# Routing tokens group by group and sending their rows to per-expert regions with indirect DMA, in place of a routing stage with selection matmuls

## The chip, the cores and the metric

The kernel runs on one core of one Trainium2 chip. The metric is the device time of one execution in microseconds (us). The engines named below are PE (TensorE, matmuls and transposes), PEld (its weight loads), DVE (VectorE), ACT (ScalarE), POOL (GpSimd, which also issues the indirect DMAs) and SP (SyncE, which issues all other DMAs). Each engine works through its own list of instructions in order and waits on semaphores. TensorE's clock has two levels, 1.2 and 2.4 GHz; the profile gives the granted clock as a share of the full one.

## What is computed

An attention block is followed by a mixture-of-experts block, on 4 batches of 2048 tokens with 256 features (8192 tokens). Cut to what matters:

```python
x = x + layernorm(attn(layernorm(x)))     # 16 heads; the 16x16 attention is over feature channels
u = layernorm(x); h = layernorm(u) * ln_g + ln_b           # 8192 tokens
logits = h @ Wr                                             # 7 routed experts
top_vals, top_idx = top_k(logits, 2); gates = softmax(top_vals)
idx = top_idx.T.reshape(-1)               # all first choices, then all second choices
pos = running count of earlier entries with the same expert; keep = pos < 732
xe[e, pos] = h[token]                     # 7 experts x 732 slots, the rest is dropped
ye = (silu(xe @ W1) * (xe @ W3)) @ W2     # 256 -> 1024 -> 256 per expert
routed[token] += ye[e, pos] * gate
shared = (silu(h @ W1s) * (h @ W3s)) @ W2s                  # all tokens
x = x + layernorm(routed + shared)
```

The order of the queue matters: an expert's 732 slots are filled by first choices over all 8192 tokens, and then by second choices.

## The kernel before

**Tiles and stages.** Tokens go in 16 groups of 512 (4 tiles of 128 rows; `GT` = 4), 4 groups per batch (`GB`). Every FFN matmul is done as three (high times low parts; `three`, lines 975 to 977). The stages, in order of time:

1. Attention of batch 0 alone (the opening).
2. A loop of three rounds, `Fori(1, B)`: in round b the shared FFN of the four groups of batch b-1 (four *chunks*, each with 8 steps m = 0..7) runs beside the attention of batch b.
3. Two more shared chunks (12 and 13), with the last steps of the attention of batch 3 and then the routing of all tokens.
4. 14 expert chunks (7 experts, two parts of 3 tiles each), whose rows are fetched by `gather` and whose results are added into `y_scratch` by `scatter`.
5. The two held shared chunks (14 and 15), beside the last layernorm, which goes on to the end.

**What sets the order.** A timetable written by hand. A round has 64 *places*: each of the 32 steps m has an even place (after `up(m)` on PE, after the product `act` on DVE) and an odd one (after `down(m-2)` on PE, after `low(m-1)` on DVE). `timetable` says at which place each step of the attention stands, `attend` issues it on each engine that has a part in it, and `LEAD` = 8 moves it: place p of a batch's timetable is place p + 8 of the round, and places 56 to 63 stand at the start of the next round. Per group q the timetable has x_stats, x_norm, x_turn0, x_low0, x_turn1, x_gram at 4q+1 to 4q+7; then the channel attention (m_gram at 20 to m_low at 37, with m_turn at 22, m_sym at 23, m_times_wqk at 24); then o_mix, o_stats, o_norm, o_add, u_stats, u_norm, u_turn0, u_turn1, u_route at 38+4q plus 0, 1, 3, 4, 6, 9, 10, 11, 12.

**Names that the change and the steps below touch.** The step keys "m_turn" and "m_sym" are on DVE `m_sum` (line 1248) and `m_sym` (line 1253): they sum the Gram matrix into `gf`, the first half of buffer `u`. PE's `m_times_wqk` (line 1015) reads that. `x_rstd` (line 655) and `x_part` (line 660) are POOL's parts of x_stats and x_low0, `x_norm` (line 1226) needs the former. `u_norm` (line 1325) writes the normed rows to `u`; SP stores them to `u_scratch` (`store_u`, line 499). `u_route` makes the logits on PE (line 1077) and copies them on DVE to `lg` (line 1332). The product `act` is line 1358, `act_lo` line 1351, the low part of a chunk's input line 1345.

**Routing before.** After all logits are there, the places after the attention in chunks 12 and 13 hold it (`route`): DVE takes the best two experts, counts, scans and positions over 448 columns (lines 1399 to 1463); PE's `count` adds up; then 32 blocks follow, each with two comparisons on DVE (`select`, lines 1475 and 1477), two products on POOL (lines 696, 697) and four fp32 matmuls on PE (line 1179), which together build a table of token number and gate per slot. `indices` (lines 1483 to 1489) reads it out, and only then `gather` (line 713) can fetch the first expert's rows. `scatter` is line 737. POOL also makes the six low parts of the first expert's weights (`low_piece`, line 651).

## Time and profile before

| what | value |
|---|---|
| median of 3 runs | 1268.76 us (1264.95 to 1269.63) |
| the profiled execution | 1270.08 us, its span 1268.3 us |
| PE busy | 1128.9 us, 89% |
| DVE busy | 724.9 us, 57% |
| ACT busy | 519.3 us, 41% |
| POOL busy | 391.4 us, 31% |
| mean granted clock | 0.941 |
| shares of the chain that ended last | PE 72%, DVE 9%, issue 8%, POOL 6%, ACT 3%, DMA 2% |

Busy PE is not PE at its peak: matmuls are pipelined and overlap in the records, so a matmul's own duration is longer than the distance to the next. In the timelines and in the chain times are us from the start of the span; ns stand where "min/median/max" is written. A bracket at the end of a timeline row says how long the engine was idle before it and what released it. Waits that are named are inferred from semaphores.

### The profile page before, as it was taken

To read this page: it belongs to the slowest core of one execution; us is meant where nothing else is said; L and a number is where in the kernel's file an instruction comes from. 1 tells how busy PE (TensorE), PEld (TensorE's weight loads), DVE (VectorE), ACT (ScalarE), POOL (GpSimd) and SP (SyncE) were. 2 spreads that over 40 slices of the span, in tenths; PEclk is the share of its full clock that TensorE was granted. 3 is DMA by queue.
4 is the path that set the end of the run, shared out by engine and by line. 5 is a ranking of instruction groups with operands and counts; after the bars stand their busy time and mean duration, and the time that the engine had idled before them with its cause. 6 is when DMAs were issued, how large, how long until landed. Compare 5 with 4: busy or idle time off the path is not lost.

```text
span 1268.3 us, 20395 instructions
## 1 busy us (share of the span) xinstructions
PE 1128.9 (89%) x6932; PEld 1033.2 (81%) x6932; DVE 724.9 (57%) x1541; ACT 519.3 (41%) x916; POOL 391.4 (31%) x321
## 2 busy tenths in 40 slices
PE   3557999999999999999998698999999999999760
PEld 2456888988888888888887597999999999998650
DVE  4445684464764564845667994445354454454885
ACT  2313343434434344343444212545455455453543
POOL 4523120131210230300312485144343434213554
PEclk9566999999999999999998898999999999999985
DMA  4206212044110044110353103244253242255773
GB/s 141 83 17 226 74 51 67 13 145 177 52 52 30 34 151 151 67 51 17 103 180 100 34 1 111 81 119 113 47 129 91 73 124 54 42 163 163 237 260 130
DMA packets 84004, 125.38 MB, mean 99 GB/s; under 512 B 8645, under 2 KB 68553, under 8 KB 83921
## 3 DMA queue, kind: packets, MB, share of 16 engines
q1 hardware_dynamic: 73728, 113.80, 27.0%
q0 software_dynamic: 10192, 10.52, 4.9%
q8 instruction: 47, 0.77, 0.3%
q14 instruction: 37, 0.30, 0.1%
HBM read 76.30 MB, written 47.98 MB: 98 GB/s over the span
## 4 chain that ended last, share of the span: by engine, by line
PE 72%; DVE 9%; issue 8%; POOL 6%; ACT 3%; DMA 2%; SPq 1%; POOLq 0%; ACTq 0%; DVEq 0%
PE bank L975 21%; PE bank L976 21%; PE bank L977 21%; PE bank L997 2%; PE bank L1077 2%; POOL sb_t_scale L772 2%; DVE sb_st L1206 1%; PE bank L1179 1%; PE bank L1069 1%; DVE sb_x L1477 1%; POOL sb_x L436 1%; ACT sb_ln_o L817 1%; PE bank L987 1%; DVE sb_act L1358 1%; PE bank L1015 1%
## 5 line engine op out<-in xcount | busy, mean ns | idle before, releaser
L1358 DVE TENSOR_TENSOR sb_act<-bank,sb_act 128x512 f32<-128x512 f32 (+2 forms) x240 | 148.7, 620 | 406.5 <-PE bank L977 365.8
L975 PE MATMUL bank<-sb_h_hi,sb_wup_lo 128*128 128x512 f32 (+2 forms) x960 | 354.8, 370 | 18.1 <-DVE sb_h_lo L1345 9.1
L976 PE MATMUL bank<-sb_h_lo,sb_wup_hi 128*128 128x512 f32 (+2 forms) x960 | 351.0, 366 | 0.0
L977 PE MATMUL bank<-sb_h_hi,sb_wup_hi 128*128 128x512 f32 (+2 forms) x960 | 349.6, 364 | 0.0
L899 ACT ACTIVATE sb_act<-bank 128x512 f32<-128x512 f32 (+2 forms) x240 | 130.1, 542 | 477.0 <-PE bank L977 434.2
L975 PE MATMUL bank<-sb_wdn_hi,sb_act_lo 128*128 128x256 f32 (+1 forms) x848 | 252.6, 298 | 24.4 <-DVE sb_act_lo L1351 22.4
L977 PE MATMUL bank<-sb_wdn_hi,sb_act_hi 128*128 128x256 f32 (+1 forms) x848 | 241.2, 284 | 0.0
L976 PE MATMUL bank<-sb_wdn_lo,sb_act_hi 128*128 128x256 f32 (+1 forms) x848 | 241.0, 284 | 0.0
L975 PEld LDWEIGHTS bank<-sb_h_hi,sb_wup_lo 128*128 128x128 f32 x960 | 183.9, 192 | 36.6 <-issue 11.9
L977 PEld LDWEIGHTS bank<-sb_h_hi,sb_wup_hi 128*128 128x128 f32 x960 | 182.9, 191 | 22.0
L976 PEld LDWEIGHTS bank<-sb_h_lo,sb_wup_hi 128*128 128x128 f32 x960 | 183.9, 192 | 16.3
L1351 DVE TENSOR_TENSOR sb_act_lo<-sb_act,sb_act_hi 128x512 fp32r<-128x512 f32 (+2 forms) x240 | 181.6, 757 | 13.2 <-ACT sb_act_hi L871 12.5
L975 PEld LDWEIGHTS bank<-sb_wdn_hi,sb_act_lo 128*128 128x128 f32 (+1 forms) x848 | 161.1, 190 | 32.7 <-DVE sb_act_lo L1351 31.1
L976 PEld LDWEIGHTS bank<-sb_wdn_lo,sb_act_hi 128*128 128x128 f32 (+1 forms) x848 | 161.8, 191 | 1.5
L977 PEld LDWEIGHTS bank<-sb_wdn_hi,sb_act_hi 128*128 128x128 f32 (+1 forms) x848 | 161.4, 190 | 0.0
L871 ACT ACTIVATE sb_act_hi<-sb_act 128x512 fp32r<-128x512 f32 (+2 forms) x240 | 136.4, 569 | 1.8 <-DVE sb_act L1358 1.8
L737 POOL DMA_INDIRECT y_scratch<-sb_ysb,sb_scur x42 | 76.7, 1827 | 161.2 <-ACT sb_ysb L888 126.7
L665 POOL TENSOR_TENSOR sb_rstdB<-sb_veB,sb_mhalf 128x4 f32<-128x4 f32 x16 | 16.2, 1015 | 231.9 <-DVE sb_veB L1305 231.9
L713 POOL DMA_INDIRECT sb_rows<-u_scratch,sb_gcur x42 | 46.7, 1112 | 57.2 <-PE bank L1093 38.9
L660 POOL TENSOR_TENSOR sb_wdn_hi<-sb_xn,sb_wdn_hi 128x1024 fp32r<-128x1024 f32 x16 | 38.2, 2389 | 57.4 <-ACT sb_wdn_hi L785 57.4
L655 POOL TENSOR_TENSOR sb_rstd<-sb_veA,sb_mhalf 128x4 f32<-128x4 f32 x16 | 16.1, 1008 | 103.0 <-DVE sb_veA L1217 103.0
L670 POOL TENSOR_TENSOR sb_x<-sb_ln_o,sb_x 128x1024 f32<-128x1024 f32 x16 | 38.1, 2381 | 30.4 <-ACT sb_ln_o L817 30.4
(195 smaller groups left out, 1452.5 us busy)
## 6 DMA issues: line engine op xcount, KB each, us to landing
sb_xin<-in_L_ffn_W_dram SPq DMA_DIRECT2D x28, 512.0 KB
sb_xin<-in_L_attn_x_dram SPq DMA_DIRECT2D x16, 512.0 KB, 3.6
sb_x<-in_L_attn_x_dram SPq DMA_DIRECT2D x16, 512.0 KB, 5.1
x_scratch<-sb_x SPq DMA_DIRECT2D x16, 512.0 KB, 5.7
u_scratch<-sb_u SPq DMA_DIRECT2D x16, 512.0 KB, 3.2
hT_scratch<-sb_hr SPq DMA_DIRECT2D x16, 512.0 KB, 2.8
sb_hfull<-hT_scratch SPq DMA_DIRECT2D x16, 512.0 KB, 3.9
y_scratch<-sb_ysb SPq DMA_DIRECT2D x14, 512.0 KB, 2.8
```

The costliest lines, as they stand in the source:

```text
L660: v.tensor_tensor(xx[:, :, 1, :], xn[:, :, :], xx[:, :, 0, :].bitcast(F32), ALU.subtract).then_inc(xlo_ok, 1)
L670: v.tensor_tensor(x2[:, q % 2, :, :], ln_o[:, :, :], x2[:, q % 2, :, :], ALU.add).then_inc(x2_ok, 1)
L713: pool.indirect_dma_start(rows[0:w, part, t, :], None, u_d, bass.IndirectOffsetOnAxis(ap=gcur[0:w, part, t:t + 1], axis=0)).then_inc(gathe ...
L737: pool.indirect_dma_start(y_d, bass.IndirectOffsetOnAxis(ap=scur[0:w, part, t:t + 1], axis=0), ysb[0:w, part, t, :], None, compute_op=ALU. ...
L772: v.tensor_tensor(t_scale[g % 2], veA[:, :], mhalf[:, :], ALU.pow).then_inc(t_rstd, 1)
L871: s.activation(act_hi[:, m % 4, 0:c.w], act[:, m % 2, 0:c.w], ACT.Copy).then_inc(ahi_ok, 1)
L899: s.activation(act[:, m % 2, 0:c.w], a[:, 0:c.w], ACT.Silu).then_inc(silu_ok, 1)
L975: t_.matmul(o, a_lo, b_hi, start=start, stop=False, skip_group_check=True)
L976: t_.matmul(o, a_hi, b_lo, start=False, stop=False, skip_group_check=True)
L977: return t_.matmul(o, a_hi, b_hi, start=False, stop=stop, skip_group_check=True)
L1351: v.tensor_tensor(act_lo[:, m % 4, 0:c.w], act[:, m % 2, 0:c.w], act_hi[:, m % 4, 0:c.w].bitcast(F32), ALU.subtract).then_inc(alo_ok, 1)
L1358: v.tensor_tensor(act[:, m % 2, 0:c.w], bank[(4 if c.wide and m % 2 else 0) + 1][:, 0:c.w], act[:, m % 2, 0:c.w], ALU.mult).then_inc(act_o ...
```

## The change

Routing is done per group of 512 tokens, beside the attention. Three steps are new in the timetable. DVE's `u_route` picks both choices of its 4 tiles right after the logits and writes the difference of the two values into column `GAP` of the group's rows; `u_norm` writes the token number into column `TOK` (rows are now 258 wide). PE's `u_count` (place 52 + 4q) counts with 11 small bf16 matmuls, and DVE's `u_slot` (same place) turns the counts, with a running `carry`, into a row number in `sent_scratch`, which has a region of 768 rows per expert and choice. POOL's `u_send0` to `u_send3` then send each tile's 128 rows twice, with one indirect DMA per tile and choice: 8 per group. These stand at places 57, 61, 84 and 88 (plus the tile's number) for the groups 0 to 3 of a batch. The timetable now reaches place 119, so that the last two groups' sends of a batch stand at places 28 to 35 of the next round.

The selection stage, its tables and the store of `u` go. `indices` shrinks to four small operations; an expert's slots read first the region of first choices, and from its end on that of second choices. The gate is computed per expert part from `GAP` (`exps` on POOL, `gates` on DVE), the scatter's targets from `TOK`. `sent_scratch` is first filled with rows that carry a spare token number: 15 DMAs on SP's queue in the opening. Group q's normed rows stand in four buffers (`early`, the two halves of `rows`, `u`) instead of one. x_turn0, x_turn1, u_turn0 and u_turn1 now share one PSUM bank in the rounds. The low parts of the first expert's weights move from POOL to DVE.

```diff
@@ timetable
-                             ("u_norm", 9), ("u_turn0", 10), ("u_turn1", 11), ("u_route", 12)):
+                             ("u_norm", 9), ("u_turn0", 10), ("u_turn1", 11), ("u_route", 12), ("u_count", 14),
+                             ("u_slot", 14)):
                 timetable[38 + 4 * q + at].append((name, q))
+        for q, at in enumerate((57, 61, 84, 88)):
+            for t in range(GT):
+                timetable[at + t].append((f"u_send{t}", q))
@@ SP, the opening
+                if place == CLEAR_AT[0]:
+                    sp.dma_start(sent_d[2 * E * ROOM:, :].rearrange("(n p) w -> p n w", p=P),
...
+                if place in CLEAR_AT:
+                    sp.dma_start(sent_t[CLEAR_AT.index(place)], zrow[:, :].rearrange("p (a w) -> p a w", a=1
+                                 ).broadcast_to([P, ST, UW])).then_inc(none_in, 16)
@@ POOL
+            def u_send(t):
+                def step(b, q):
+                    if t == 0:
+                        pool.wait_ge(r_slot, OPEN + b * GB + (q + 1))
+                        if isinstance(b, int) and b == 0 and q == 0:
+                            pool.wait_ge(none_in, (2 * E + 1) * 16)
+                        elif q > 0:
+                            pool.wait_ge(sent[q - 1], b * SENT + SENT)
+                        else:
+                            pool.wait_ge(sent[GB - 1], b * SENT)
+                        pool.sem_inc(pool_go, 1)
+                    for c in range(2):
+                        pool.indirect_dma_start(sent_d, bass.IndirectOffsetOnAxis(ap=sendto[:, q, t, c:c + 1], axis=0),
+                                                u[q][:, t, :], None).then_inc(sent[q], 16)
+                return step
...
-            for j in range(PIECES):
-                low_piece(1, j, 1, stage_later)
-
-            pool.wait_ge(r_slots, 1)
-            for n in range(NBLK):
...
-                v.tensor_tensor(selB[:, r, :, 0, :], selE[:, r, :, :], along(tokid[:, cut], NC), ALU.mult)
-                v.tensor_tensor(selB[:, r, :, 1, :], selE[:, r, :, :], along(gates[:, c, cut], NC),
-                                ALU.mult).then_inc(r_sel, 1)
@@ PE
+            def u_count(b, q):
+                pe.wait_ge(r_oh, b * GB + (q + 1))
+                t_.matmul(counts, earlier[:, :], oh[:, :, :, :].rearrange("p t c e -> p (t c e)"),
+                          start=True, stop=False, skip_group_check=True)
...
+                for t in range(1, GT):
+                    for s in range(t):
+                        t_.matmul(counts[:, t * 2 * E:(t + 1) * 2 * E], onesb[:, :], of[s],
+                                  start=False, stop=False, skip_group_check=True)
+                for t in range(GT):
+                    ins = t_.matmul(totals, onesb[:, :], of[t], start=False, stop=(t == GT - 1),
+                                    skip_group_check=True)
...
-                    for t in range(RB):
-                        ins = t_.matmul(bank[6][:, 0:2 * NC], selA[:, n % SR, t, :],
-                                        selB[:, n % SR, t, :, :].rearrange("p a c -> p (a c)"),
...
@@ DVE, m_sum
                 dve.wait_ge(m_act, OPEN + b * MA + 1)
-                dve.wait_ge(u_out, OPEN + b * (16 * GB))
+                if not (isinstance(b, int) and b == 0):
+                    dve.wait_ge(sent[GB - 1], b * SENT)
@@ DVE, u_route (new part) and u_slot
+                for c in range(2):
+                    ch.link(v.tensor_reduce(best[:, c, :], lg[:, :, :], AX.X, ALU.max))
+                    ch.link(v.tensor_tensor(same[:, :, :], lg[:, :, :], over_e(best[:, c, :]), ALU.is_equal))
+                    ch.link(v.tensor_tensor(same[:, :, :], same[:, :, :], of_e, ALU.mult))
+                    ch.link(v.tensor_reduce(first[:, :], same[:, :, :], AX.X, ALU.max))
+                    ins = v.tensor_tensor(oh[:, :, c, :], same[:, :, :], over_e(first[:, :]), ALU.is_equal)
...
+            def u_slot(b, q):
...
+                dve.wait_ge(r_cnt, g + 1)
+                ch.link(v.tensor_tensor(place_of[:, :, :, :], counts.rearrange("p (t c e) -> p t c e", c=2, e=E), over_t,
+                                        ALU.add))
...
+                ch.link(v.tensor_reduce(pos[:, :, :], place_of[:, :, :, :], AX.X, ALU.add))
+                ch.step(v.tensor_copy(sendto[:, q, :, :], pos[:, :, :]))
+                ch.settle()
+                dve.sem_inc(r_slot, 1)
@@ DVE, per expert part
+            def gates(c):
...
+                ch.link(v.tensor_scalar(gsum[:, :], ex, 1.0, None, ALU.add))
+                ch.link(v.reciprocal(grec[:, :], gsum[:, :]))
...
@@ DVE, chunks 12 and 13
-            def select(n):
...
-                v.tensor_tensor(selE[:, r, :, :], across(colid[:, :], NC), along(slotcol[:, c, cut], NC),
-                                ALU.is_equal).then_inc(r_selE, 1)
-                v.tensor_tensor(selA[:, r, :, :], across(slot1[:, :], P), along(slotm[:, c, cut], P),
-                                ALU.is_equal).then_inc(r_selA, 1)
```

Where the sends stand is told by the order of the instructions. POOL, in a round, from the end of x_low0 of the batch's last group to the first step after it. Before:

```order
L655 TENSOR_TENSOR sb_rstd<-sb_veA,sb_mhalf 128x4 [waits a_var]
L659 REGISTER_ALU
L660 TENSOR_TENSOR sb_wdn_hi<-sb_xn,sb_wdn_hi 128x4x256 [waits xhi_ok]
L665 TENSOR_TENSOR sb_rstdB<-sb_veB,sb_mhalf 128x4 [waits b_var]
L669 ISA [waits lno_ok]
```

and with the change:

```order
L683 TENSOR_TENSOR sb_rstd<-sb_veA,sb_mhalf 128x4 [waits a_var]
L687 REGISTER_ALU
L688 TENSOR_TENSOR sb_wdn_hi<-sb_xn,sb_wdn_hi 128x4x256 [waits xhi_ok]
L707 REGISTER_ALU
L716 DMA sent_scratch<-sb_rows,sb_sendto 11776x258 [waits r_slot,sent1]
L716 DMA sent_scratch<-sb_rows,sb_sendto 11776x258 x7
L707 REGISTER_ALU
L716 DMA sent_scratch<-sb_u,sb_sendto 11776x258 [waits r_slot,sent2]
L716 DMA sent_scratch<-sb_u,sb_sendto 11776x258 x7
L693 TENSOR_TENSOR sb_rstdB<-sb_veB,sb_mhalf 128x4 [waits b_var]
```

Sixteen indirect DMAs, for groups 2 and 3 of the batch before, now stand between x_low0 and the next step, and group 3's wait until group 2's have landed (`sent2`).

DVE, in a round, around the sum of the Gram matrix into `u`. Before:

```order
L1358 TENSOR_TENSOR sb_act<-bank,sb_act 128x512 [waits b_ps,silu_ok]
L1244 ISA
L1245 ISA [waits m_act]
L1248 TENSOR_TENSOR sb_u<-sb_ln_o 128x512 [waits ut_ps,u_out]
L1351 TENSOR_TENSOR sb_act_lo<-sb_act,sb_act_hi 128x512 [waits dn_done,ahi_ok]
L1253 TENSOR_TENSOR sb_u<-sb_u,bank 128x512 [waits m_pe]
```

and with the change:

```order
L1478 TENSOR_TENSOR sb_act<-bank,sb_act 128x512 [waits b_ps,silu_ok]
L1286 ISA
L1288 REGISTER_ALU [waits m_act]
L1291 TENSOR_TENSOR sb_u<-sb_ln_o 128x512 [waits ut_ps,sent3]
L1454 TENSOR_TENSOR sb_act_lo<-sb_act,sb_act_hi 128x512 [waits dn_done,ahi_ok]
L1294 ISA
L1295 REGISTER_ALU [waits m_chain]
L1296 TENSOR_TENSOR sb_u<-sb_u,bank 128x512 [waits m_pe]
```

The operations are the same; the first now waits for `sent3`, the landing of group 3's sends of the batch before, where it waited for the store of `u`.

## Rows read from the trace of the kernel before

**Rows 1.** Windows: from:to, length, busy time of each engine, clock, DMA share, GB/s.

```profile
295.20:473.80 178.60, 174.42 (x1063) 154.92 (x1061) 102.96 (x243) 72.60 (x122) 32.62 (x20) 1.00 0.25 84
446.90:459.90 13.00, 13.00 (x93) 12.09 (x93) 8.94 (x28) 5.18 (x10) 4.86 (x3) 1.00 0.62 203
652.40:786.10 133.70, 112.87 (x699) 100.68 (x697) 102.93 (x159) 35.89 (x55) 68.36 (x80) 0.92 0.20 67
```

**Rows 2.** Timeline of DVE, chunks 12 and 13: start, length, line, operation.

```profile
655.29 0.69 DVE L1358 TENSOR_TENSOR sb_act<-bank,sb_act 128x512 f32<-128x512 f32 x1 [3.47 <-PE bank L977]
775.89 0.69 DVE L1358 TENSOR_TENSOR sb_act<-bank,sb_act 128x512 f32<-128x512 f32 x1 [3.04 <-PE bank L977]
```

**Rows 3.** The chain that ended last, two stretches: start, length, what.

```profile
377.48 0.12 PE bank L975
...
381.66 1.73 PE bank L1015 x8
...
779.86 2.67 DMA sb_rows<-u_scratch,sb_gcur
782.58 0.56 PE bank L1093 x3
...
787.06 0.69 PE bank L975
```

**Rows 4.** Forms of one line's instructions: ns min/median/max, first and last start.

```profile
L1077 PE MATMUL bank<-sb_wr,sb_hr x256: 169/255/378, 97.4 to 669.9; 128*128 128x7 f32 x128
L1160 PEld LDWEIGHTS bank<-sb_oh,sb_onesb x2: 96/96/96, 679.7 to 694.5; 128*128 128x128 bf16 x2
```

**Rows 5.** The page's groups of indirect DMAs on POOL: busy, mean ns, idle before.

```profile
L737 POOL DMA_INDIRECT y_scratch<-sb_ysb,sb_scur x42 | 76.7, 1827 | 161.2 <-ACT sb_ysb L888 126.7
L713 POOL DMA_INDIRECT sb_rows<-u_scratch,sb_gcur x42 | 46.7, 1112 | 57.2 <-PE bank L1093 38.9
```

**Rows 6.** Timeline of POOL in a round, at chunk 12 and in the experts.

```profile
304.48 1.02 POOL L674 TENSOR_TENSOR sb_rstd<-sb_ve,sb_mhalf 128x4 f32<-128x4 f32 x1 [12.93 <-DVE sb_ve L1317]
323.85 1.01 POOL L655 TENSOR_TENSOR sb_rstd<-sb_veA,sb_mhalf 128x4 f32<-128x4 f32 x1 [18.35 <-DVE sb_veA L1217]
362.12 2.40 POOL L660 TENSOR_TENSOR sb_wdn_hi<-sb_xn,sb_wdn_hi 128x1024 fp32r<-128x1024 f32 x1 [4.36 <-ACT sb_wdn_hi L785]
658.10 1.02 POOL L674 TENSOR_TENSOR sb_rstd<-sb_ve,sb_mhalf 128x4 f32<-128x4 f32 x1 [9.87 <-DVE sb_ve L1317]
783.08 0.95 POOL L713 DMA_INDIRECT sb_rows<-u_scratch,sb_gcur  x1 [0.30 <-issue]
832.19 0.58 POOL L705 COPY sb_gcur<-sb_gidx 128x3 uint32<-128x3 uint32 x1 [4.30 <-DMA y_scratch<-sb_ysb,sb_scur]
```

**Rows 7.** Timeline of DVE in a round, and small chained operations in `indices`.

```profile
325.82 1.38 DVE L1226 TENSOR_SCALAR sb_xn<-sb_xin,sb_mv,sb_rstd 128x256 f32<-128x256 f32 x4
377.76 0.68 DVE L1248 TENSOR_TENSOR sb_u<-sb_ln_o 128x512 f32<-128x512 f32 x1
378.96 0.68 DVE L1253 TENSOR_TENSOR sb_u<-sb_u,bank 128x512 f32<-128x512 f32 x1
772.19 0.20 DVE L1486 TENSOR_TENSOR sb_tabe<-sb_tabe,sb_spare 128x42 f32<-128x42 f32 x1
772.43 0.20 DVE L1488 TENSOR_TENSOR sb_tabe<-sb_tabe,sb_table 128x42 f32<-128x42 f32 x1
```

**Rows 8.** Timeline of PE: the first x_turn0 of a round.

```profile
328.53 0.60 PE L987 MATMUL bank<-sb_ident,sb_xn 128*128 128x128 f32 x4
```

**Rows 9.** Windows after PE's wait for the first expert's rows; columns as in rows 1.

```profile
790.00:792.00 2.00, 2.00 (x7) 2.00 (x7) 0.56 (x1) 0.00 (x0) 0.57 (x2) 0.50 1.01 302
792.00:794.00 2.00, 2.00 (x12) 2.00 (x12) 0.04 (x1) 0.91 (x2) 0.00 (x0) 0.94 0.99 313
```

**Rows 10.** Timeline of the opening: SP issues the residual loads, POOL first uses one.

```profile
48.94 0.93 SPq L485 DMA_DIRECT2D sb_x<-in_L_attn_x_dram  x2
85.37 2.36 POOL L670 TENSOR_TENSOR sb_x<-sb_ln_o,sb_x 128x1024 f32<-128x1024 f32 x1 [2.24 <-ACT sb_ln_o L817]
```

**Rows 11.** Window with SP's queue full; columns as in rows 1.

```profile
298.00:302.00 4.00, 4.00 (x21) 3.39 (x22) 0.34 (x1) 2.24 (x3) 0.00 (x0) 1.00 0.99 299
```

More of the change, by code:

```diff
@@ L246, in sandwich_kernel @@
         u_ok = sem("u_ok")
-        u_out = sem("u_out")
+        sent = [sem(f"sent{i}") for i in range(GB)]
         ut_ps = sem("ut_ps")
@@ L350, in held_chunks, with stored @@
         def held_chunks(body, between=lambda place: None):
[L352 to L353 removed]
+            seq = [expert_chunk(E - 1, 1, 1)] + [held_chunk(h) for h in range(HELD)] + [None]
+            for h in range(HELD):
+                body(seq[h], seq[h + 1], seq[h + 2], lambda place: between(2 * FM * h + place))
+        def stored(s):
+            return sum((n + HELD) % 2 == s for n in range(FIRST))
         NCH = NG + 2 * E
@@ L559, in _ @@
             b = B - 1
-            load_h(b, 1)
-            for place in range(PLACES - LEAD, PLACES):
-                attend(steps, place, b)
             for k in range(4):
@@ L565, in _ @@
                 sp.sem_inc(sp_go, 1)
-            for j in range(PIECES):
+            for j in range(3):
+                load_piece(1, j, [W1[0], W3[0]], W2[0], stage_later)
+            if HELD < GB - 1:
+                load_h(b, 1)
+            for place in range(PLACES - LEAD, TIMES):
+                attend(steps, place, b)
+            for j in range(3, PIECES):
                 load_piece(1, j, [W1[0], W3[0]], W2[0], stage_later)
@@ L597, in _ @@
                 sp.dma_start(last_y[k], last_view(y_d[0:T, :], k)).then_inc(t_y[k], 16)
+            for h in range(2, HELD):
+                load_held(h)
             for g in range(NG):
@@ L743, in _ @@
             gather(0, 1)
+            exps(0, 0, 0)
+            exps(0, 1, 0)
             release(0, 0)
@@ L1491, in route @@
-            def route(place):
-                for step, c in routing.get(place, ()):
-                    step(c)
-                for n in blocks_at(place):
-                    select(n)
-                if place == R_IDX:
-                    indices()
-            cs = last_chunks()
-            body(None, cs[0], cs[1], lambda place: beside_last(steps, route, place))
-            body(cs[0], cs[1], None, lambda place: beside_last(steps, route, 2 * FM + place))
-            low(cs[1], FM - 1)
@@ new lines, in route @@
+            def route(place):
+                if place % 2 and 5 <= place < 5 + 2 * PIECES:
+                    j = (place - 5) // 2
+                    if j == 4:
+                        dve.wait_ge(sent[0], B * SENT)
+                    low_piece(1, j, 1, stage_later)
+                if place == INDEX_AT:
+                    indices()
+            cs = [None] + last_chunks() + [None]
+            for j in range(1, len(cs) - 1):
+                body(cs[j - 1], cs[j], cs[j + 1], lambda place: beside_last(steps, route, 2 * FM * (j - 1) + place))
```

516 lines of the change are left out of this document (250 added, 266 removed).

## The prediction, made before the changed kernel ran

> **What bounds the kernel now.** I read the busy times first: PE is busy for 89% of the span, no other engine for more than 57%. Then the windows: inside a round PE is busy in 174.4 of 178.6 us at full clock while DVE has 103 us of work, but in the stretch from the end of the rounds to the first expert chunk (133.7 us) PE has 112.9 us, DVE 102.9 us, and the granted clock falls to 0.92 [rows 1]. So the kernel is bound by PE nearly everywhere, and in the routing stretch by DVE, POOL and PE in turn. The chain of waits says how that stretch ends: the gather of the first rows lands, PE turns them, and the first expert matmul starts at 787.06 [rows 3]. The question is what that stretch becomes without its selection, and what its work costs where PE was full.
>
> **Term 1, the routing stretch: -52.5 us.** One step m of a shared chunk costs PE 4.18 us (381.66 less 377.48: one `down` and one `up` with nothing between) [rows 3]. The first product of chunk 12 is at 655.29, the last of chunk 13 at 775.89 [rows 2]. Between them lie 15 steps, 62.7 us. The tail of the attention adds two sets of logits (16 records each, about 1.7 us for a set: 0.105 us apart, with a median of 255 ns for one because they overlap [rows 4]), eight transposes (0.7 us) and three new counts (0.8 us each, below), together 6.5 us; for DVE running late I add 2 us. So the last product comes at 726.5. From there to the first expert matmul it was 11.2 us, of which about 3 us was PE waiting for the gather (rows landed at 782.5); the rest stays: 734.6. Gain 787.06 less 734.6, 52.5 us. What hides the sends here: POOL is free from 659.1 [rows 6], four groups at 13.3 us each (term 2) end at 712, and gather takes 6 us more, so the rows are there at 718, before PE asks at about 729. DVE has the six low parts of the weights as new work (about 1.2 us each, one per step), in steps where it has over 2 us free.
>
> **Term 2, the sends: +48 us.** The trace has no plain indirect write. Nearest are the gather, 0.95 us where nothing disturbs it [rows 6] and 1.112 us in the mean of 42, and the accumulating scatter, 1.827 us [rows 5]; 0.30 us lies between two [rows 6]. I take the gather's mean, since both move a row without arithmetic, and the accumulation is what the scatter has more: 1.41 us per send, 11.3 us per group. A group must land before the next starts: 1.7 us after the gather's issue (landing 2.67 us after its start) [rows 3], 4.3 us after the scatter's [rows 6]; I take 2.0. A group is then 13.3 us (bounds 11.7 and 21.3).
>
> The Trainium skill, page "SBUF — State Buffer", section "SBUF: two separate sides", says that a DVE operation in a two-port mode keeps GpSimd from writing descriptors until it ends. The spread between 0.95 us and the mean of 1.112 us is the only thing here that fits it; by the undisturbed price this term would be about 7 us smaller. No run here separates the two.
>
> First place, the start of a round: POOL is free at 305.5, sends groups 0 and 1 until 305.5 + 13.3 + 11.3 = 330.1, and only then does x_rstd, which stood at 323.85 [rows 6]. x_norm waits for that, 1.4 us long [rows 7], and x_turn0 on PE stood at 328.53 [rows 8]. It would start at 332.5; new work ahead moves everything here by some 2 us, so 2 us are lost, 6 us in three rounds.
>
> Second place, which decides: POOL ends the last x_part at 364.5 [rows 6], sends groups 2 and 3 (row order above) and they have landed at 364.5 + 26.6 = 391.1. `m_sum` on DVE stood at 377.76 and now waits for that. Queued behind it on DVE are act_lo and m_sym, and `m_times_wqk` on PE, at 381.66 [rows 3], needs m_sym. The three take 1.9 us (0.6 us from start to start) [rows 7], so PE goes on at 393.0 and has stood for 11.3 us. After an idle PE the clock is at its lower level: PE's dense work at 787.06 ran at 0.50, the level of 1.2 GHz, until about 792 [rows 9], 5 us of work at half speed, 2.6 us lost. Together 13.9 us, in three rounds 41.7 us.
>
> **Term 3, routing beside the FFN: +21.5 us.** A count is 11 bf16 matmuls with 11 weight loads. Bounds from two rows: 0.105 us apart like the logits' fp32 records [rows 4], 1.16 us; half that, as the bf16 weight load takes 96 ns where the fp32 one takes 190, 0.58 us. I take 0.8 us. On DVE a group gets 10 new operations in u_route and 8 in u_slot at 0.24 us from start to start (0.2 us each, chained) [rows 7], and two small copies: 4.6 us. DVE has 8.94 us of work in 13.0 us in the fullest window [rows 1], so the sum is 13.5 us where PE's becomes 13.8: both full, and DVE in order. Where logits stand ahead of act_lo and u_norm, I find u_norm about 0.7 us after the point where PE wants to transpose. I take 1.0 us per group. 1.8 us times 12 groups in the rounds is 21.6 us (bounds 0.6 and 3.5 per group: 7 and 42).
>
> **Term 4, the opening: +5.5 us.** There the path runs through DVE, so the two u_route chains (2.4 us each) and part of a u_slot count: 5 us. SP fills `sent_scratch` ahead of the residual loads: 13 of the 15 DMAs, 10240 rows of 1032 bytes, 10.6 MB. At the 299 GB/s of a full queue [rows 11] that is 35 us; they start when the residual loads did, 48.9, and these then land at about 86 to 88, where 85.4 was wanted [rows 10]. 0.5 us, bounds 0 and 15 (a rate a third lower).
>
> **Nothing: the experts.** Per part POOL gets one `pow` (1 us) and DVE one copy and four small operations, 1.2 us of 25 us. PE has two PSUM banks per product there and is busy without a break; the cover is DVE's half-idle time. Bounds -2 and +6. The rest of the tail is untouched.
>
> **Sum.** 1268.3 - 52.5 + 48 + 21.5 + 5.5 = 1290.8 us of span; the execution was 1.8 us longer than its span, so 1292.6, and 1.3 us less against the median of the runs: 1292.
>
> **Rivals.**
> (a) The stretch gained outweighs the rest (faster). Mechanism: the wait of m_sum. Its loss per round is 364.5 + two groups + 1.9 - 381.7. With the lowest price (1.25 us per send, 1.7 us to land) that is 8.1 us without a fall of the clock; with counts and chains at 0.6 us per group and 2 us in the opening the sum is -55 + 24 + 7 + 2 = -22, 1247. The point from which it decides: with my other terms the whole breaks even at a loss of 6 us per round, a send of 1.08 us with its gap. For it: 0.95 us stands in the trace. Against: even that with its gap is 1.25.
> (b) A plain indirect write costs what the accumulating one does (1.83 + 0.3 us, 4.3 to land, 21.3 per group). Then m_sum loses 27.3 + 2.6 us per round, x_norm about 18, and the sends of chunks 12 and 13 end at 744, so that the first rows come 20 us after PE could take them: 52.5 becomes 32. Sum -32 + 90 + 54 + 21.5 + 5.5: about 1407. For it: same direction, SBUF to memory. Against: packets and bytes are the same, only the addition differs.
> (c) The middle is worse than taken: DVE is the bound in all 16 groups (3.5 us each) or the filling holds up the residual loads. +20 or +15: about 1310.
>
> **How the numbers follow.** Forecast (1275 to 1305) 0.47; (a), 1245 to 1275, 0.25; (b) 0.10; (c), with sends half-way between the two prices, 0.18. The range 1252 to 1340 leaves out (b) and the low end of (a). About 0.5%, 6 us, is what a measurement can tell from no change. Faster by more than that (below 1262) is most of (a), 0.20; same (to 1275) the rest of it and the forecast's lower edge, 0.12; slower 0.68.
>
> **What would show it.** Right: in each round DVE's sum into `sb_u` idle for 9 to 14 us behind an indirect DMA, PE idle as long ahead of its line, and the clock low after it; sends of 1.0 to 1.2 us, 128 of them; a round of 193 to 203 us in place of 178.6; 80 us from chunk 12 to the first expert. Wrong: a send near 1.8 us, an experts' stretch that grows, or PE full through the middle of a round.

## The result, and the profile after

The changed kernel took 1326.17 us (median of 4, 1324.05 to 1328.51), the kernel before 1267.53 us (its three earlier runs and one more): a ratio of 1.046, 95% interval 1.044 to 1.049, slower by 58.6 us. The forecast was 1292 us. The direction held and the time lies in the range, but the loss is more than twice the 24 us forecast. The experiments below split it in two: run on two other chips, the same program takes 1299.5 and 1301.9 us, so 24 to 27 us of the 58.6 are not in the program alone. Two single executions, one of the kernel before and one of `e4_again`, took over 1860 us at a granted clock of 0.56 and are left out of all times. I therefore show two traces of it, *after* (the first measurement, span 1324.4 us) and *c0* (the same program on another chip, span 1300.7 us).

To see where time goes I compare the starts of the same `up` product on PE in two traces. In the kernel before, the first products of the three rounds start at 117.1, 298.0 and 476.6, that of chunk 12 at 652.3, the first expert product at 787.06 [rows 3], one late in the experts at 1089.2. A *mark* below is the first `up` product of any step m; it shifts by what it falls further behind the kernel before, counted from the mark ahead of it. Differences of the stretches to before, in us:

| kernel | opening | three rounds | of it at m_sum | chunk 12 to experts | experts | tail | span |
|---|---|---|---|---|---|---|---|
| forecast | +5.5 | +69.2 | +41.7 | -52.5 | 0 | 0 | +22.5 |
| after | +9.9 | +89.7 | +35.5 | -45.9 | +2.1 | +0.1 | +56.0 |
| c0 | +10.5 | +71.5 | +35.4 | -52.5 | +1.8 | +1.1 | +32.4 |

The tail is what is left to the span's end. Windows of after (round 2 and the last stretch), then of c0; the columns are those of rows 1:

```profile
336.20:544.70 208.50, 183.85 (x1102) 160.03 (x1102) 117.06 (x327) 73.00 (x123) 64.25 (x52) 0.95 0.24 82
751.90:840.80 88.90, 77.51 (x473) 66.55 (x471) 42.82 (x109) 32.97 (x52) 45.59 (x46) 0.98 0.42 138
```

```profile
331.90:533.60 201.70, 180.99 (x1102) 158.30 (x1102) 117.35 (x327) 73.18 (x124) 64.61 (x52) 0.97 0.25 84
734.30:816.60 82.30, 75.71 (x474) 65.54 (x472) 42.69 (x109) 33.08 (x52) 45.17 (x46) 0.99 0.47 149
```

A round was 178.6 us with PE busy for 174.4 [rows 1]. In c0 it is 201.7 us, and PE stands for 20.7 of them. DVE has 14 us more work in 84 more instructions, POOL 32 us more, the sends. The last stretch was 133.7 us and is 82.3: the gain that was forecast is there.

**The wait that decided.** c0, round 2: the timelines of POOL, DVE and PE (start, length, what; in brackets the idle time before it and what ended it):

```profile
402.94 2.39 POOL L688 TENSOR_TENSOR sb_wdn_hi<-sb_xn,sb_wdn_hi 128x1024 fp32r<-128x1024 f32 x1 [4.47 <-ACT sb_wdn_hi L836]
418.81 0.96 POOL L716 DMA_INDIRECT sent_scratch<-sb_u,sb_sendto  x1 [2.70 <-issue]
427.66 0.96 POOL L716 DMA_INDIRECT sent_scratch<-sb_u,sb_sendto  x1 [0.30 <-issue]
430.11 0.69 DVE L1291 TENSOR_TENSOR sb_u<-sb_ln_o 128x512 f32<-128x512 f32 x1 [11.25 <-DMA sent_scratch<-sb_u,sb_sendto]
432.05 3.78 PE L1067 MATMUL bank<-sb_wqk,sb_u 128*128 128x256 f32 x8 [9.35 <-DVE sb_u L1296]
```

The last x_part ends at 405.33. Groups 2 and 3 go out and have landed at 430.1, 24.8 us later, and only then may DVE sum the Gram matrix into `u`. PE stands for 9.35 us, and behind it the eight matmuls of L1067 take 3.78 us, where rows 3 have 1.73: the clock is at its lower level (0.54 in the window from 432 to 437, 1.00 in the next five). Together the same product comes 11.9 us later.

**The price of a send.** The row of c0's trace for half of the sends, those out of buffer `rows` (ns min/median/max, first and last start), and three rows of its timelines:

```profile
L716 POOL DMA_INDIRECT sent_scratch<-sb_rows,sb_sendto x64: 956/961/1741, 153.2 to 784.3; - x64
```

```profile
414.59 0.69 DVE L1454 TENSOR_TENSOR sb_act_lo<-sb_act,sb_act_hi 128x512 fp32r<-128x512 f32 x1
414.92 1.19 POOL L716 DMA_INDIRECT sent_scratch<-sb_rows,sb_sendto  x1 [0.30 <-issue]
415.20 1.22 DVE L1448 TENSOR_TENSOR sb_h_lo<-sb_hfull,sb_h_hi 128x1024 fp32r<-128x1024 f32 x1
```

105 of the 128 sends take 0.96 to 0.99 us, the mean is 1.01. Of the 23 longer ones 19 begin while DVE subtracts one SBUF tile from another (act_lo, the low part of a weight): here act_lo ends at 415.28 and the send at 416.11, 0.83 us later, and that distance is the same in 16 of them (0.91 in three). The next subtraction, which starts 0.28 us into the send, does not hold it. Of the other sends under such a subtraction three begin in its last 0.14 us, and three begin 0.02 us behind its start and are not held. The eleven sends that begin under DVE's product out of PSUM (L1478) all take 0.96 us. The Trainium skill, page "SBUF — State Buffer", section "SBUF: two separate sides", has this as a lock on a port pair, held by whichever starts first, and names DVE operations with two SBUF inputs among those that take it, against a GpSimd operation that reads SBUF. The 19 held sends and the eleven agree with that, the three at the start of a subtraction do not. The 19 cost 6.3 us of POOL's time in all.

**The opening.** SP's and POOL's timelines, c0:

```profile
49.52 29.23 SPq L555 DMA_DIRECT2D sent_scratch<-sb_zrow  x12
79.36 3.47 SPq L497 DMA_DIRECT2D sb_x<-in_L_attn_x_dram  x2
90.46 2.34 POOL L698 TENSOR_TENSOR sb_x<-sb_ln_o,sb_x 128x1024 f32<-128x1024 f32 x1 [7.51 <-DMA sb_x<-in_L_attn_x_dram]
```

The residual loads went out at 48.94 before and POOL used one at 85.37 [rows 10]. Now twelve clearing DMAs hold SP for 29 us, and POOL waits 7.5 us for the load.

**The turn of a round.** c0, from round 1 to round 2, ACT, DVE and PE:

```profile
318.91 1.93 ACT L869 ACTIVATE sb_ln_o<-bank,sb_nbiasB,sb_rstdB 128x256 f32<-128x256 f32 x4 [2.28 <-DVE sb_nbiasB L1352]
321.36 0.69 DVE L1478 TENSOR_TENSOR sb_act<-bank,sb_act 128x512 f32<-128x512 f32 x1 [2.48 <-ACT sb_act L954]
321.97 0.18 DVE L1385 COPY sb_lg<-bank 128x28 f32<-128x28 f32 x1
325.24 0.16 DVE L1399 TENSOR_TENSOR sb_rows<-sb_best 128x4 f32<-128x4 f32 x1
325.31 0.68 DVE L1454 TENSOR_TENSOR sb_act_lo<-sb_act,sb_act_hi 128x512 fp32r<-128x512 f32 x1
326.05 0.58 PE L1026 MATMUL bank<-sb_wdn_hi,sb_act_lo 128*128 128x256 f32 x1 [4.24 <-DVE sb_act_lo L1454]
336.75 0.66 PE L1122 MATMUL bank<-sb_ident,sb_rows 128*128 128x128 f32 x4 [1.03 <-ACT sb_hr L878]
346.63 0.66 PE L1122 MATMUL bank<-sb_ident,sb_u 128*128 128x128 f32 x4 [1.57 <-DVE sb_u L1375]
```

DVE's slot chain ahead (314.16 to 315.90) makes the norm's bias late (ACT waits 2.28 us for it), ACT's silu comes behind that, DVE's product behind the silu, and then DVE works through the choice of experts, from 321.97 to 325.40, before act_lo. PE waits 4.24 us for it, and its granted clock is 0.50 from 326.0 to 330.5, where it was 1.00 at this place before. Before, the same two waits were 0.45 and 0.27 us.

In c0 the marks shift by 4.0, 3.4 and 5.1 us at the three turns. At the next mark they shift by 1.2 to 1.6 us: the second transposes of a group wait 1.03 us for the bank that they share with the first. Two marks further the shift is 2.1 us in each round: at 346.63 PE waits for u_norm, which stands on DVE behind the next choice of experts. A count adds 0.4 us. At the start of the attention two transposes share a bank again, and the shift is 1.2 to 1.3 us.

### The profile page after: what moved, and what is told of

Its sections match the earlier page's. It is cut to its first block, busy times and chain, and to the rows that moved or that the text cites. A ratio compares the mean times of both kernels' runs of the same rounds, so it can differ in the third digit from the quotient of the medians.

```text
span 1324.4 us, 20814 instructions
## 1 busy us (share of the span) xinstructions
PE 1121.6 (85%) x6848; PEld 1013.3 (77%) x6848; DVE 718.9 (54%) x1847; ACT 517.0 (39%) x913; POOL 471.3 (36%) x380
## 4 chain that ended last, share of the span: by engine, by line
PE 36%; issue 6%; POOL 5%; DVE 2%; DMA 1%; ACT 1%; another core or an unknown queue 0%; POOLq 0%; ACTq 0%; DVEq 0%; SPq 0%
PE bank L1026 12%; PE bank L1028 11%; PE bank L1027 11%; POOL sb_t_scale L823 2%; POOL sent_scratch L716 1%; POOL sb_x L448 1%; PE bank L1161 1%; POOL y_scratch L782 0%; DMA sb_xin<-in_L_ffn_W1s_dram 0%; DMA y_scratch<-sb_ysb,sb_scur 0%; DVE sb_act_lo L1454 0%; DVE sb_st L1248 0%; DMA sb_xin<-y_scratch 0%; POOL sb_rows L448 0%
## 5 line engine op out<-in xcount | busy, mean ns | idle before, releaser
L1478 DVE TENSOR_TENSOR sb_act<-bank,sb_act 128x512 f32<-128x512 f32 (+2 forms) x240 | 148.8, 620 | 406.2 <-PE bank L1028 308.5
L1028 PE MATMUL bank<-sb_h_hi,sb_wup_hi 128*128 128x512 f32 (+2 forms) x960 | 353.3, 368 | 0.0
L1028 PE MATMUL bank<-sb_wdn_hi,sb_act_hi 128*128 128x256 f32 (+1 forms) x848 | 244.0, 288 | 0.0
L1454 DVE TENSOR_TENSOR sb_act_lo<-sb_act,sb_act_hi 128x512 fp32r<-128x512 f32 (+2 forms) x240 | 175.1, 729 | 17.8 <-ACT sb_act_hi L923 13.0
L751 POOL DMA_INDIRECT sb_rows<-sent_scratch,sb_gcur x42 | 48.6, 1157 | 104.3 <-DVE sb_scur L1444 47.2
L716 POOL DMA_INDIRECT sent_scratch<-sb_rows,sb_sendto x64 | 67.4, 1054 | 34.1 <-issue 24.3
L702 POOL TENSOR_TENSOR sb_rstd<-sb_ve,sb_mhalf 128x4 f32<-128x4 f32 x16 | 19.9, 1245 | 97.9 <-DVE sb_ve L1360 97.9
```

The lines of the kernel that those rows point to most:

```text
L716: pool.indirect_dma_start(sent_d, bass.IndirectOffsetOnAxis(ap=sendto[:, q, t, c:c + 1], axis=0), u[q][:, t, :], None).then_inc(sent[q], 16)
L751: pool.indirect_dma_start(rows[0:w, part, t, :], None, sent_d, bass.IndirectOffsetOnAxis(ap=gcur[0:w, part, t:t + 1], axis=0)).then_inc(ga ...
L1028: return t_.matmul(o, a_hi, b_hi, start=False, stop=stop, skip_group_check=True)
L1454: v.tensor_tensor(act_lo[:, m % 4, 0:c.w], act[:, m % 2, 0:c.w], act_hi[:, m % 4, 0:c.w].bitcast(F32), ALU.subtract).then_inc(alo_ok, 1)
L1478: v.tensor_tensor(act[:, m % 2, 0:c.w], bank[(4 if c.wide and m % 2 else 0) + 1][:, 0:c.w], act[:, m % 2, 0:c.w], ALU.mult).then_inc(act_o ...
```

## The experiments

Edits are to the changed kernel, but for two that add a part of the change to the kernel before. All times have the kernel before beside them (1267.0 to 1267.9 us).

### The changed kernel again, on other chips

> The changed kernel once more, unedited. Three edits that have nothing in common (the Gram's buffer, DVE's order, the order of the clearing) all removed the same losses, some 6 us at 311 us and 5 us at 504 us of the kernel before's time, where signals of PE came up to 5 us late in the trace of the changed kernel. Theory (that lateness belongs to the execution, the chip or what else ran, not to the edits): 1300 us, the time of e3_clear_later and the 8 us of the opening. Rival (it belongs to the program as it is laid out): 1326 us again, with the late signals in the trace.

c0: 1299.54 us, ratio 1.024 (1.021 to 1.027).

> The changed kernel, unedited, a third time. Theory (the 26 us between the first measurement, 1326 us, and the second, 1299.5 us, come with where it ran, not with the program): 1300 us again, or 1326 us again with PE's signals late in the trace while POOL sends, and nothing between. Rival (it varies from one execution to the next): single times spread between the two.

c1: 1321.92 us, ratio 1.041 (1.039 to 1.043), single times 1319.64 to 1326.45.

> The changed kernel, unedited, a fourth time, to mark whether this place has PE's signals late (1322 to 1326 us) or on time (1300 us).

c2: 1301.87 us, ratio 1.027 (1.024 to 1.030). So the program has two levels, and which one it takes goes with the place: each chip was used in one batch of runs, so chip and moment are not told apart. The later runs fell on five chips. On one, c1's, every execution is at the upper level, as in the first measurement, whose chip may be the same one; c0 and c2 have the lower level on two others, and on the remaining two the edited kernels show what c0 shows. The kernel before took the same time on all. What differs in the trace: waits that no instruction of another engine explains by its end. The list of waits (engine, line, what it waited for, us in total, times, longest), all such rows of after, then of c1:

```profile
ACT sb_act L954 <- remote: 19.5, 3, 8.3
ACT sb_hr L878 <- remote: 18.1, 4, 5.7
DVE sb_place_of L1406 <- remote: 10.0, 5, 3.5
DVE sb_act L1478 <- remote: 6.4, 2, 4.3
```

```profile
ACT sb_act L954 <- remote: 22.9, 3, 9.1
ACT sb_hr L878 <- remote: 18.3, 4, 5.8
DVE sb_act L1478 <- remote: 7.2, 2, 4.9
DVE sb_place_of L1406 <- remote: 5.8, 4, 2.1
```

54.0 and 54.2 us, and c0 and c2 have no such row, nor has any trace of the edited kernels but that of `e7_turn`, taken beside c1. All of these lines wait for a signal of PE, the semaphore update by which it tells that it is done. One place of after, then the same place of c0:

```profile
349.11 0.24 PE L1145 MATMUL bank<-sb_oh,sb_onesb 128*128 128x14 bf16 x4
350.95 0.66 PE L1122 MATMUL bank<-sb_ident,sb_u 128*128 128x128 f32 x4 [1.59 <-issue]
352.92 0.22 DVE L1406 TENSOR_TENSOR sb_place_of<-bank,sb_carry 128x56 f32<-128x56 f32 x1 [1.44 <-remote]
355.93 0.78 ACT L878 ACTIVATE sb_hr<-bank,sb_bcol,sb_gcol 128x512 f32<-128x512 f32 x1 [5.72 <-remote]
356.76 1.11 PE L1122 MATMUL bank<-sb_ident,sb_u 128*128 128x128 f32 x4 [3.73 <-ACT sb_hr L878]
```

```profile
344.81 0.24 PE L1145 MATMUL bank<-sb_oh,sb_onesb 128*128 128x14 bf16 x4
346.63 0.66 PE L1122 MATMUL bank<-sb_ident,sb_u 128*128 128x128 f32 x4 [1.57 <-DVE sb_u L1375]
347.08 0.21 DVE L1406 TENSOR_TENSOR sb_place_of<-bank,sb_carry 128x56 f32<-128x56 f32 x1
347.47 0.78 ACT L878 ACTIVATE sb_hr<-bank,sb_bcol,sb_gcol 128x512 f32<-128x512 f32 x1 [1.58 <-PE bank L1122]
```

In c0 ACT reads the transposes 0.18 us after their end (347.29). In after they end at 351.61 and ACT starts at 355.93, 4.3 us later; DVE starts on the counts 3.6 us after theirs. PE itself worked on until 353.03. These places all lie in or just behind a stretch in which POOL issues sends (here 345.87 to 355.77). They are not spread evenly over it: 45 of the 46 such waits in after, c1 and `e7_turn` end 7.1, 8.5 to 8.7, 9.9 to 10.1 or 11.3 to 11.6 us after the start of the group's first send. So the lateness is tied to the row of sends itself and not only to its time; how is open.

### The wait of m_sum

```diff
-        gf, tsb = by_tile(own[:, 0:KC * D]), by_tile(own[:, KC * D:2 * KC * D])
+        gf, tsb = by_tile(early[:, 0:KC * D]), by_tile(early[:, KC * D:2 * KC * D])
...
-                    dve.wait_ge(sent[GB - 1], b * SENT)
+                    dve.wait_ge(sent[0], b * SENT)
```

(`u_norm`'s wait for the readers of the Gram sum moves from group 3 to group 0 with it.)

> The changed kernel with the Gram sum's two tiles laid into the send buffer of group 0 in place of that of group 3, so that DVE's m_sum waits for the landing of group 0's sends, done long before, and no longer for group 3's. Theory (the wait of m_sum is worth what the trace of the changed kernel shows, 11.7 to 12.1 us a round with the fall of the clock): 3 x 11.8 = 35 us less, 1291 us; PE has no idle over 1 us at L1067 and the rounds are about 197 us long. Rival (the sends of groups 2 and 3 now run beside the short steps between PE, DVE and ACT of the attention's middle and slow these): less than half of it comes back, 1310 us or more.

e1: 1265.65 us, ratio 0.998 (0.997 to 0.999): 34 us less than c0. At m_sum the rounds lose 0.1 us in all, where c0 loses 35.4; the rest of the rounds (37.1) and the last stretch (-52.4) are as in c0. The expected 1291 was reckoned from the 1326 with late signals; as a difference, 35 us expected stand against 34. DVE in round 2:

```profile
404.48 0.68 DVE L1291 TENSOR_TENSOR sb_early<-sb_ln_o 128x512 f32<-128x512 f32 x1
```

It waits for nothing. The sends of groups 2 and 3 now run beside the short steps of the attention, and the rest of the rounds loses 37.1 us where c0 loses 36.1: the rival is out.

### Half the sends

```diff
-    SENT = 2 * GT * 16
+    SENT = GT * 16
...
-                    for c in range(2):
+                    for c in range(1):
```

> The changed kernel with the second choice's sends left out (four sends a group in place of eight; rows of the second choice are missing, so part of the routed sum is left out). A group takes 5.1 us less, so m_sum waits 10.1 us less a round: 30 us for that alone. Theory (the rest of the loss in the rounds is DVE's chains): the phase of the groups' output and routing loses as much as in the changed kernel, 18 us a round, 1295 us. Rival (the sends themselves disturb that phase, PE's signals come late while POOL issues them): it loses 3 to 5 us a round less, 1280 to 1285 us.

e4: 1277.31 us, ratio 1.009 (1.007 to 1.011). The rounds lose 15.4 us at m_sum, 20.0 less than c0 and not 30, and 32.8 elsewhere. Neither forecast is right. The 10.1 us were taken from the issue alone; POOL and DVE in round 2:

```profile
407.65 0.96 POOL L716 DMA_INDIRECT sent_scratch<-sb_u,sb_sendto  x1 [0.31 <-issue]
414.21 0.69 DVE L1291 TENSOR_TENSOR sb_u<-sb_ln_o 128x512 f32<-128x512 f32 x1 [5.27 <-DMA sent_scratch<-sb_u,sb_sendto]
```

The last send lands 5.6 us after its issue where it took 1.5 us in c0. SP's load of `hfull` and two residual loads go out at 406.7 and 407.3, and the shorter row of sends now ends inside them; that this is why it lands late is likely, but no run takes the loads away. And at the start of the attention, where c0 loses 1.2 to 2.0 us a round, this kernel loses 0.0: there `x_rstd` stood right behind the sends of group 1. That is the first place of term 2.

Twice more, to see whether few sends keep signals on time:

> The changed kernel with the second choice's sends left out (part of the routed sum is left out), a second time. It gave 1277 us with PE's signals on time. Theory (lateness needs a row of many sends): where e5_again has late signals this has few, 1277 to 1283 us. Rival (any indirect DMA brings them): half of the changed kernel's 24 us, 1289 us.

> The changed kernel with the second choice's sends left out (part of the routed sum is left out), beside c2_after. On two places with signals on time it gave 1277 and 1280 us. If c2_after's signals are late: theory (lateness builds up over a row of many sends) 1277 to 1283 us, few late signals; rival (any indirect DMA brings them) 1289 us or more. If they are on time: 1277 to 1280 us again, and nothing follows.

`e4_again` 1277.76 and `e4_third` 1275.14 us. Both chips had signals on time, so nothing follows from either.

### DVE's chains and the shared bank, each added to the kernel before

Twelve chained operations on 28 columns behind the copy of a group's logits, eight more two places later:

```diff
+                for n in range(12):
+                    ch.link(v.tensor_scalar(pad[:, :], onesb[:, 0:GT * E], 1.0, None, ALU.mult))
```

> The kernel before with twelve chained operations of 28 columns added on DVE behind the copy of each group's logits, and eight more two places later, at the places where the change has its choice and its slots (no result uses them). Theory (DVE in order is what costs at the turn of a round, 4.1 us at one place and 1.6 us behind it): 5 to 6 us a round and 2 in the opening, 20 us, 1288 us. Rival (they find DVE idle): 1270 us.

b2: 1303.39 us, ratio 1.028 (1.025 to 1.030), 36 us slower: +2.9 us in the opening, +28.0 in the rounds, +2.0 in the last stretch. DVE and PE at the turn:

```profile
299.37 3.61 DVE L1340 TENSOR_SCALAR sb_pad<-sb_onesb 128x28 f32<-128x28 bf16 x12
303.01 0.69 DVE L1363 TENSOR_TENSOR sb_act_lo<-sb_act,sb_act_hi 128x512 fp32r<-128x512 f32 x1
303.76 0.58 PE L979 MATMUL bank<-sb_wdn_hi,sb_act_lo 128*128 128x256 f32 x1 [5.27 <-DVE sb_act_lo L1363]
```

PE waits 5.27 us for act_lo, behind the twelve. The theory's mechanism holds, its size was too low: 9.3 us a round, 2.3 us a group. They go at two places, 4.4 to 6.3 us at the turn and 3.8 to 4.2 us where u_norm is late. At the second the changed kernel itself loses only 2.1 us, so b2 is not the changed kernel's own price.

Both transposes in bank 7, the second waiting for the reader of the first:

```diff
+                    pe.wait_ge(hT_ok, OPEN + b * (2 * GB) + (2 * q + k))
...
-                        ins = t_.transpose(bank[6 + k][:, t * P:(t + 1) * P], u[:, t, k * P:(k + 1) * P], ident[:, :])
+                        ins = t_.transpose(bank[7][:, t * P:(t + 1) * P], u[:, t, k * P:(k + 1) * P], ident[:, :])
```

> The kernel before with one part of the change alone: both transposes of a group (of the attention's input in rounds 1 to 3, of the normed output in all) in PSUM bank 7, the second waiting until the first has been read. Theory (one bank for both costs what the runs with edits still show late in their rounds, 2.1 us in the middle and 2.3 to 3.1 us at the start of the attention): 4 us in each of three rounds, 12 to 15 us in all, 1281 us. Rival (PE has other work between the two, and only late DVE work makes it wait): 0 to 3 us, 1269 us.

b1: 1275.74 us, ratio 1.006 (1.004 to 1.008): 6.4 us in the rounds, half of what was expected, 2.1 us a round (1.5, 3.1 and 1.8). Most is lost where no product stands between the two transposes, with the same wait as in c0 at 336.75:

```profile
306.61 0.66 PE L1076 MATMUL bank<-sb_ident,sb_u 128*128 128x128 f32 x4 [1.03 <-ACT sb_hr L830]
```

### Moving the chains

```diff
-                             ("u_norm", 9), ("u_turn0", 10), ("u_turn1", 11), ("u_route", 12), ("u_count", 14),
-                             ("u_slot", 14)):
+                             ("u_norm", 9), ("u_turn0", 10), ("u_turn1", 11), ("u_route", 12)):
...
+            for name, at in (("u_pick", 13), ("u_count", 15), ("u_slot", 15)):
```

(`u_pick` is DVE's part of u_route.)

> The changed kernel with DVE's choice of experts one place later (place 13 of a group in place of 12, behind act_lo and u_norm in DVE's order) and count and slot one place later too (15). Theory (DVE works in order, and its chain of twelve small operations ahead of act_lo is what makes PE stand 4.24 us at 330 us and the clock fall behind it): 6 us less in each of three rounds and in the last stretch, 1302 us. Rival (what costs in this phase is the sends of groups 0 and 1 and the one bank for both transposes, the DVE chains are covered): at most 2 us a round, 1320 us or more.

e2: 1297.57 us, ratio 1.024 (1.022 to 1.025), not to be told from c0. Both forecasts were reckoned from the 1326 with late signals. As differences they are 6 us and at most 2 us a round; the rounds lose 29.7 us besides m_sum where c0 loses 36.1, 2.1 us a round less. That is the rival's size, but not by its reason: what comes back is mainly the 2.1 us at u_norm, now ahead of the choice (0.3 to 0.4 us are left), so the chains were not covered. The wait for act_lo at the turn is still 2.84 us. DVE's order matters, but a place later is no cover.

### The clearing behind the residual loads

```diff
-        CLEAR_AT = range(14, 14 + 2 * E)
+        CLEAR_AT = range(27, 27 + 2 * E)
```

> The changed kernel with the fourteen clearing DMAs issued from place 27 on, behind the first two residual loads, in place of 14. Theory (the residual loads land late because the clearing is ahead of them in the queue): PE's place that stood 8.0 us later than before comes back whole, 1318 us. Rival (the clearing only moves its collision to the later loads and stores of the opening): 1324 us or more.

e3: 1294.48 us, ratio 1.022 (1.020 to 1.024). The opening is +5.6 us in place of +10.5 (8.3 to 11.3 in the traces without this edit); POOL has its residual at 84.76:

```profile
50.44 0.93 SPq L497 DMA_DIRECT2D sb_x<-in_L_attn_x_dram  x2
51.95 31.27 SPq L555 DMA_DIRECT2D sent_scratch<-sb_zrow  x12
84.76 2.36 POOL L698 TENSOR_TENSOR sb_x<-sb_ln_o,sb_x 128x1024 f32<-128x1024 f32 x1 [2.24 <-ACT sb_ln_o L869]
```

The first logits come 0.6 us later than before where c0 has 6.3, but 5.0 us go from there to the first `up` product, of which b2's chains alone show 3.4. So of the opening the clearing costs 3 to 6 us, and about 3 of the other 5 are DVE's chains.

### The three edits together, and one more

> The three edits together: Gram's tiles in group 0's send buffer, choice, count and slot one place later, clearing behind the first residual loads. Theory (they mend different places and add up): from e1's 1265.7, 2 to 5 us less in the opening and 1 to 2 us less in each of four phases of the groups' output, 1256 us, faster than both kernels. Rival (the losses are the same time counted twice, PE waits for the next thing): 1264 us.

e5: 1255.76 us, ratio 0.990 (0.988 to 0.993), 12 us faster than the kernel before.

> The three edits together, a second time, beside the two kernels that follow. Theory: 1256 us if PE's signals come on time in its trace, 1275 to 1280 us if they come late, and nothing between (the changed kernel's two levels, 1300 and 1322 to 1326 us).

`e5_again`: 1256.27 us, ratio 0.992 (0.990 to 0.994), again with signals on time. The edits add up (trace of the first of the two): opening +5.1, rounds +30.9, last stretch -53.0. PE still waits 1.35 us for act_lo at the turn. With the choice of group 1 one place later still:

> The three edits together, and the choice of group 1 one place later still, so that at the turn of a round it no longer stands on DVE ahead of the low part that PE's second-last product waits for (a wait of 1.35 us and a slower clock behind it in the trace of the three edits). Theory: half of the 6 us lost at the turn come back, 3 us in three rounds and the last stretch, 1247 us where the changed kernel gives 1300. Rival (the wait moves to the next place): 1255 us.

> The three edits with the choice of group 1 one place later, a second time. It gave 1273 us where PE's signals were late, and has no number for signals on time. Theory (it takes 3 us out of each turn of a round): 1245 to 1250 us if this place has signals on time, 1273 us if late. Rival (the wait only moves): the same as e5_again.

e7: 1273.0 us on a chip with late signals (c1 took 1321.92 there), 1260.61 us with signals on time, 4 us slower than `e5_again`. The wait for act_lo at the turn is gone (0.25 us), but PE's count now waits for the choice, and everything behind it:

```profile
321.31 0.23 PE L1139 MATMUL bank<-sb_oh,sb_earlier 128*128 128x56 bf16 x1 [3.89 <-DVE sb_oh L1395]
```

The rival was right: the wait moved, and grew.

### Spaced sends

```diff
+                        v.tensor_tensor(pace[:, :], ones[:, 0:GT], mhalf[:, :], ALU.pow).then_inc(pace_s, 1)
```

> The three edits with one POOL operation of about 1 us behind each send, so that a group's sends stand some 2.5 us apart in place of 1.27, and a group takes 20 us in place of 10. Theory (PE's signals are late where sends follow one another closely): if e5_again shows late signals, this one shows none or few, and is faster than e5_again in spite of its longer groups; if e5_again shows none, it is 0 to 5 us slower, since the start of the attention on POOL is reached later. Rival (what counts is how long POOL is busy with sends): as many late signals as e5_again or more, and slower.

e8: 1323.09 us, ratio 1.044 (1.041 to 1.046), against 1256.27: 67 us slower where 0 to 5 were expected. The chip had signals on time, so it says nothing of those. But it shows the first place of term 2 at full size. With 2.31 us from send to send the row ends behind the point where `x_rstd` is wanted; POOL and PE, round 2:

```profile
374.80 1.00 POOL L687 TENSOR_TENSOR sb_rstd<-sb_veA,sb_mhalf 128x4 f32<-128x4 f32 x1
377.59 1.11 PE L1044 MATMUL bank<-sb_ident,sb_xn 128*128 128x128 f32 x4 [14.88 <-DVE sb_xn L1274]
```

PE stands for 14.88 us, and 16.7 to 17.7 us are lost in each round; the gather of the first expert's rows comes late as well (PE waits 20.9 us for it).

## Why the prediction was right or wrong

The loss was forecast as 24 us and is 58.6. Two steps failed. The larger, 24 to 27 us, is a term that the sum does not have: PE's signals coming late while POOL sends. It was put at nothing without a word on it, and its cause is open. The other is term 3, the work beside the FFN: 31.6 us for 21.5. With signals on time the parts are off by +10.1 (term 3), -8.1 (term 2), +5.0 (term 4) and +2.9 us (experts and tail). That their sum is off by only 9.9 us is luck: term 2 was too high by nearly as much as term 3 was too low.

**Term 1, -52.5 us.** Right: -52.5 in c0, -52.8 in c2. The exactness is partly luck, since the counts are cheaper and DVE's lateness dearer than taken. With late signals it is -45.9.

**Term 2, +48 us.** Right in mechanism and place, somewhat too high. A send is 0.96 us (1.01 in the mean) and not 1.112, from start to start 1.27, a group in the rounds 9.8 to 10.6 us; the two landings take 2.7 and 1.5 us, together what 2.0 each gives. The wait of DVE was forecast at 9 to 14 us and is 11.25; PE stands 9.35 where 11.3 was said, and the clock takes 2.5 where 2.6 was said. Sum 35.4 for 41.7, shown by e1. The start of the attention costs 1.2, 1.3 and 2.0 us, 4.5 in all for 6 (c0 against e4).

**Term 3, +21.5 us.** A step that failed, though inside its own bounds of 7 and 42. c0 loses 71.5 - 35.4 - 4.5 = 31.6 us there. PE's count was put at 0.8 us and is 0.4. DVE's new work was put at 4.6 us per group and is 3.6 (14.4 in a round). Its lateness was put at 1.0 us per group from a single point, u_norm. That point costs 2.1 us a round in c0; what was not seen is the turn of a round, 4.0, 3.4 and 5.1 us. Together 18.8 us, 1.6 per group; added alone to the kernel before the chains cost 2.3 (b2). At the turn a chain does not only delay what is behind it on DVE, it goes round through ACT (bias, norm, silu) and back to DVE, and PE then runs at the lower clock. And the diff puts both transposes in one bank, which I did not cost at all: 2.1 us a round alone (b1), and 2.4 to 2.9 at the marks of c0. The three measured or taken alone (28.0, 6.4, and 12 counts of 0.4, 4.8) sum to 39, more than 31.6, so they overlap; no run separates where.

**Term 4, +5.5 us.** 8.3 to 11.3 us in four traces of the same program. The rate was right (312 GB/s in the window from 52 to 80 of after), but I let the residual loads land with the clearing, at 86 to 88, while they stood behind it and landed at 90.5. 3 to 6 us for 0.5. For the chains 5 were said: without the clearing's delay the opening is 4.6 to 5.6 us longer (e3, e5), of which the chains alone show 2.9 (b2).

**The experts, 0.** +1.8, within the bounds, and 1.1 in the tail (0.2 in c2). No run asks for its cause.

**The rest.** With signals on time the sum is 32.4 us of span for 22.5 forecast, 1299.5 us for 1292. Of the late signals the trace of before showed nothing. Rival (c) named DVE and the filling as what would be worse than taken, and both were, at half the size or less. Rival (b) is out, by the price; (a) failed on the wait of m_sum, which cost far more than the 6 us a round at which it would have decided.

## What to carry to other kernels

A buffer that is lent to two uses turns the slower use into a wait of the other: count from the last queued transfer to the landing, and ask first whether another buffer is free by then. Here that one move was worth 34 us, nearly half of what the rounds lost. A chain of tiny dependent operations is priced by what it does to the loop through the other engines, not by the engine's idle share; shifting it by one place gave back 2 us a round, shifting part of it by one more moved the wait and made it longer. And a rerun on another chip belongs before an explanation: three unrelated edits that all "mend" the same loss are a sign that it isn't in the program alone.

## What the runs showed of the hardware

On one of five chips, and in the first measurement, signals of PE reached ACT and DVE up to about 4 us late by the places shown (waits of up to 9 us in the list) while POOL issued rows of indirect DMAs, and the same program took 20 to 27 us more in the median, every execution above every one on time (1319.6 and up against 1303.8 and down); on the other four no wait of that kind is in the traces. The late waits end at four distances from the first send of a group, 7.1, 8.6, 10.0 and 11.5 us, within 0.2 us, all but one of 46. What about the place or the sends brings it stays open: e4 and e8 were meant to tell number from closeness, and both fell on chips without it. The kernel without sends (before) was untouched on all. e7, which has as many sends, lost 12 us to it.

A plain indirect write of 128 rows of 1032 bytes is 0.96 us of POOL and 0.30 to the next, half of the accumulating one (1.83 [rows 5]); one that begins under a DVE subtraction of two SBUF tiles ends 0.83 us after it (16 of 19; 0.91 in three), unless it begins within 0.02 us of its start (three sends, 0.96 us).
